# A graph network kernel: the bias in halves at a later place, and the last steps of the first layer's sweep in an order of their own

## The reference, cut to what matters

```python
h = relu(layernorm(x))
msg = h[src] + edge_attr                  # layer 0
m = segment_max(msg * beta, dst)
e = exp(msg * beta - m[dst])
agg = segment_sum(msg * e, dst) / segment_sum(e, dst)
x = x + (agg @ H(phm_rule, W) + bias + h)
h = relu(layernorm(x))                    # layer 1: attention with 4 heads over wx = h @ W.T
x = x + elu(attention(h, W, a, src, dst))
```

## Time and profile before

| what | value |
|---|---|
| median of 3 runs | 2296.75 us (2295.61 to 2296.79) |
| profiled execution, its own time | 2297.38 us |
| its span in the profile | 2295.6 us |
| busy: TensorE, VectorE, ScalarE, GpSimd | 88%, 87%, 59%, 72% of the span |
| layer 0's sweep | about 43 to 1122 us |
| between the layers | 1122 to 1197 us |

### The profile page before, as it was taken

The page is one execution under the profiler, slowest core; times in us unless marked ns, Lnnn a source line. Parts: engine busy times, 40 slices in busy tenths (PEclk is TensorE's granted clock), DMA queues, the critical chain, the costliest instruction groups (busy, mean ns, idle before and its releaser), DMA issues.

```text
span 2295.6 us, 63252 instructions
## 1 busy us (share of the span) xinstructions
PE 2013.3 (88%) x15341; PEld 1806.1 (79%) x15342; DVE 1997.8 (87%) x3846; ACT 1361.5 (59%) x3479; POOL 1648.3 (72%) x1741
## 2 busy tenths in 40 slices
PE   1899999999999999998458999999999999999996
PEld 0778887888887888787458888888888888888885
DVE  7888989898989998999477888888888888888887
ACT  2566666666666666666544555555555555555555
POOL 4777777777777777777427777777777777777772
PEclk9999999999999999999677999999999999999998
DMA  7444454444444444443023333333333333333322
GB/s 209 116 132 135 131 136 131 126 131 135 131 136 131 136 129 128 131 136 99 1 62 61 61 58 59 58 59 59 59 59 59 58 59 59 58 59 58 59 60 67
DMA packets 338046, 214.22 MB, mean 93 GB/s; under 512 B 169981, under 2 KB 304502, under 8 KB 337990
## 3 DMA queue, kind: packets, MB, share of 16 engines
q0 software_dynamic: 53248, 112.57, 20.0%
q1 hardware_dynamic: 282190, 99.72, 17.3%
q10 hardware_dynamic: 2552, 1.28, 0.2%
HBM read 201.37 MB, written 10.29 MB: 92 GB/s over the span
## 4 chain that ended last, share of the span: by engine, by line
POOL 43%; issue 20%; DMA 14%; DVE 10%; PE 6%; ACT 4%; SPq 1%; POOLq 0%; ACTq 0%; DVEq 0%
POOL msg L618 23%; POOL ring_h L582 19%; DMA ring_h<-h_dram,meta_g 11%; PE sums L1229 3%; DVE sums L994 2%; DMA msg<-wx_dram,meta_g 2%; DVE seg_max L999 2%; ACT sums L749 2%; DVE onehot L978 1%; DVE prod L1129 1%; ACT acc L719 1%; PE banks L1238 1%; POOL ring_h L608 1%; PE banks L1245 1%; POOL diff L606 1%
## 5 line engine op out<-in xcount | busy, mean ns | idle before, releaser
L618 POOL DMA_INDIRECT msg<-wx_dram,meta_g x832 | 791.9, 952 | 293.5 <-issue 246.3
L582 POOL DMA_INDIRECT ring_h<-h_dram,meta_g x832 | 788.6, 948 | 260.8 <-issue 248.7
L1229 PE MATMUL sums<-onehot,prod 128*128 128x128 f32 x3312 | 688.2, 291 | 15.1 <-issue 6.1
L1229 PE MATMUL sums<-onehot,wgt 128*128 128x128 f32 x3312 | 674.1, 287 | 0.0
L1229 PEld LDWEIGHTS sums<-onehot,prod 128*128 128x128 f32 x3312 | 535.8, 204 | 47.7 <-issue 47.2
L1229 PEld LDWEIGHTS sums<-onehot,wgt 128*128 128x128 f32 x3312 | 536.7, 204 | 0.0
L719 ACT ACTIVATE acc<-sums 128x1022 f32 x412 | 422.0, 1024 | 0.2
L1238 PE MATMUL banks<-beta_ident,msg 128*128 128x128 f32 x1664 | 243.5, 290 | 91.3 <-DVE msg L1017 89.9
L749 ACT ACTIVATE sums<-ring_h 128x512 f32<-128x512 f32 x208 | 125.1, 602 | 321.7 <-DMA ring_h<-h_dram,meta_g 321.7
L1238 PEld LDWEIGHTS banks<-beta_ident,msg 128*128 128x128 f32 x1664 | 204.8, 194 | 119.7 <-issue 92.8
L1249 PEld LDWEIGHTS banks<-neg_ident,seg_max 128*128 128x128 f32 x1664 | 219.6, 192 | 100.5 <-issue 100.0
(11 more groups left out here) (162 smaller groups left out, 2806.3 us busy)
## 6 DMA issues: line engine op xcount, KB each, us to landing
msg<-in_edge_attr SPq DMA_DIRECT2D x207, 256.0 KB
flags<-flag_dram SPq DMA_DIRECT2D x52, 512.2 KB
ring_h<-h_dram,meta_g POOLq DMA_INDIRECT x832
msg<-wx_dram,meta_g POOLq DMA_INDIRECT x832
window<-wx_dram SPq DMA_DIRECT2D x832, 2.0 KB
wx_dram<-msg SPq DMA_DIRECT2D x13, 272.0 KB, 2.4
nodes<-in_x SPq DMA_DIRECT2D x6, 512.0 KB, 6.8
h_dram<-acc SPq DMA_DIRECT2D x12, 256.0 KB
```

The costliest lines, as they stand in the source:

```text
L582: pool.indirect_dma_start(hg[:, s % HRING, b, :], None, h_dram, bass.IndirectOffsetOnAxis(ap=meta_g[:, s, b:b + 1], axis=0)).then_inc(L0[" ...
L618: pool.indirect_dma_start(msg[:, s, b, :], None, wx_dram, bass.IndirectOffsetOnAxis(ap=meta_g[:, s, b:b + 1], axis=0)).then_inc(L1["gather ...
L1229: ins = pe.matmul(where[:, j, bass.ds(off, P)], what[:, slot, b, :], onehot[:, s, b, :], start=(b == 0), stop=(b == GB - 1), skip_group_ch ...
```

## The change

- The bias addition becomes a helper for either engine. GpSimd adds it to even batches (seven) and VectorE to odd ones (six). GpSimd starts when VectorE has done the last `drop` of layer 0 and no longer waits for `odd_sum`; VectorE starts behind its last product and the sign change of the matrix (L1051), once `odd_sum` is full. `finish0` waits for the half that its batch belongs to.
- The last steps of layer 0 stand in an order of their own on ScalarE, VectorE and TensorE, and the sums of the fourth last and second last group go to `spare_sums0`, banks 2 and 3.
- For that, `row_psum` moves to bank 2 and the result of `unturn0` moves from bank 2 to the bank that `row_psum` had. TensorE writes a row of zeros to bank 3 at the start, and ScalarE waits before the sweep for its own table copies.

```diff
-        row_psum = sums[:, 1, 0, :]
+        shift_psum = sums[:, 1, 0, :]
...
+        row_psum = bank[2]
+        spare_sums0, spare_sums = banks[:, 2:4, :], banks[:, 0:2, :]
...
+        def add_bias(eng, b, done):
+            t = 1 if b == NBAT - 1 else GB
+            tiles = nodes[:, b * GB:b * GB + t, :]
+            eng.tensor_tensor(tiles, tiles, bias_all[:, :].rearrange("p (a d) -> p a d", a=1).to_broadcast([P, t, D]),
+                              ALU.add).then_inc(done, 1)
...
@@ gpsimd
-            pool.wait_ge(odd_sum, NBAT // 2)
             pool.wait_ge(weights_in, 16 * W_DMA)
+            pool.wait_ge(L0["dropped"], NG)
+            straight(NBAT, [(0, even_bias)])
...
@@ scalar
-            sweep_edges(act, [(5, merge0), (0, lift0), (3, weigh0)], until=NG + 4)
+            sweep_edges(act, [(5, merge0), (0, lift0), (3, weigh0)], until=NG - 1)
+            last(weigh0, 3)
+            last(merge0, 5)
+            last(weigh0, 2)
+            last(lift0, 0)
+            last(merge0, 4)
+            last(weigh0, 1)
+            last(merge0, 3, where=spare_sums0)
+            last(weigh0, 0)
+            last(merge0, 2)
+            last(merge0, 1, where=spare_sums0)
             act.activation(spare[:, :], spare[:, :], ACT.Ln)
             last(merge0, 0)
...
@@ vector
-            sweep_edges(dve, [(0, add0), (0, one_hot0), (3, products0), (1, maxima0)])
+            sweep_edges(dve, [(0, add0), (0, one_hot0), (3, products0), (1, maxima0)], until=NG - 1)
+            last(products0, 3)
+            last(maxima0, 1)
+            last(one_hot0, 0)
+            last(add0, 0)
+            last(products0, 2)
+            last(maxima0, 0)
+            last(products0, 1)
+            last(products0, 0)
             dve.tensor_scalar(phm_neg[:, :], ...)
+            dve.wait_ge(odd_sum, NBAT // 2)
+            straight(NBAT, [(0, odd_bias)])
...
@@ tensor
-            sweep_edges(pe, [(4, sums0), (0, turn0), (2, unturn0)])
+            sweep_edges(pe, [(4, sums0), (0, turn0), (2, unturn0)], until=NG - 1)
+            last(unturn0, 2)
+            last(sums0, 4)
+            last(turn0, 0)
+            last(unturn0, 1)
+            pe.wait_ge(L0["onehots"], NG)
+            pe.wait_ge(L0["added"], NG)
+            last(sums0, 3, where=spare_sums0, free=1)
+            last(sums0, 2, free=1)
+            last(unturn0, 0)
+            last(sums0, 1, where=spare_sums0, free=1)
+            last(sums0, 0, free=1)
```

More of the change, by code:

```diff
@@ L213, in gnn_kernel @@
         bank = [banks[:, i, :] for i in range(4)]
-        own_sums, spare_sums = sums[:, 0, :, :], banks[:, 0:2, :]
+        row_psum = bank[2]
+        own_sums = sums[:, 0, :, :]
+        spare_sums0, spare_sums = banks[:, 2:4, :], banks[:, 0:2, :]
         iota_psum = bank[3][:, 0:P]
@@ L259, in gnn_kernel @@
         h_stored = sem("h_stored")
-        bias_added = sem("bias_added")
+        bias_even, bias_odd = sem("bias_even"), sem("bias_odd")
         phm_turned = sem("phm_turned")
@@ L588, in _, with even_bias @@
             pool.wait_ge(even_sum, (NBAT + 1) // 2)
-            pool.wait_ge(odd_sum, NBAT // 2)
             pool.wait_ge(weights_in, 16 * W_DMA)
[L592 to L598, removed]
+            pool.wait_ge(L0["dropped"], NG)
+            def even_bias(b):
+                if b % 2 == 0:
+                    add_bias(pool, b, bias_even)
+            straight(NBAT, [(0, even_bias)])
             def near0(b):
@@ L723, in _ @@
             act.wait_ge(blk_loaded, 16)
+            act.wait_ge(key_out, len(TABLE_BANKS))
             act.wait_ge(h_stored, 16 * NBAT)
@@ L731, in weigh0, with merge0 @@
                     act.wait_ge(L0["summed"], g - (WGT - 1))
-                act.activation(wgt[:, s % WGT, :, :], bank[2][:, :].rearrange("p (b d) -> p b d", b=GB), ACT.Exp)
+                act.activation(wgt[:, s % WGT, :, :], shift_psum.rearrange("p (b d) -> p b d", b=GB), ACT.Exp)
                 if later(g, 1):
                     act.wait_ge(L0["multiplied"], g)
-                act.activation(wgt_psum, bank[2][:, :], ACT.Exp).then_inc(L0["weighed"], 1)
+                act.activation(wgt_psum, shift_psum, ACT.Exp).then_inc(L0["weighed"], 1)
                 act.wait_ge(L0["dropped"], g + 1)
                 act.activation(scale[:, s:s + 1], drop[:, s:s + 1], ACT.Exp).then_inc(L0["factored"], 1)
-            def merge0(g, s, use):
+            def merge0(g, s, use, where=own_sums):
                 if isinstance(g, int) and g == 0:
                     act.wait_ge(odd_sum, NBAT // 2)
-                merge(g, s, use, L0, None)
+                merge(g, s, use, L0, None, where)
             def lift0(g, s, use):
@@ L1046, in _, with odd_bias @@
             link(dve.tensor_copy(iota_psum, iota_f[:, :]))
-            sweep_edges(dve, [(0, add0), (0, one_hot0), (3, products0), (1, maxima0)])
+            sweep_edges(dve, [(0, add0), (0, one_hot0), (3, products0), (1, maxima0)], until=NG - 1)
[7 more added lines that the diff above has]
+            last(products0, 0)
             dve.tensor_scalar(phm_neg[:, :], phm[:, :, :].rearrange("p j b -> p (j b)"), -1.0, None, ALU.mult
                               ).then_inc(phm_turned, 1)
+            dve.wait_ge(odd_sum, NBAT // 2)
+            def odd_bias(b):
+                if b % 2:
+                    add_bias(dve, b, bias_odd)
+            straight(NBAT, [(0, odd_bias)])
             def quotient0(b):
@@ L1065, in finish0 @@
                 dve.wait_ge(mid_out, b + 1)
-                dve.wait_ge(bias_added, b + 1)
+                dve.wait_ge(bias_odd if b % 2 else bias_even, b // 2 + 1)
                 tiles = nodes[0:rows, b * GB:b * GB + t, :]
@@ L1186, in _ @@
             pe.wait_ge(const_ready, 1)
+            pe.matmul(bank[3][:, :], zero_row[0:1, 0:P], zero_row[0:1, :], start=True, stop=True)
             def turn_table(rows_f, first, done):
@@ L1244, in unturn0 @@
                     pe.wait_ge(L0["weighed"], g)
-                pe.matmul(bank[2][:, :].rearrange("p (b d) -> p b d", b=GB), beta_ident[:, :], msg[:, s, :, 0:D],
+                pe.matmul(shift_psum.rearrange("p (b d) -> p b d", b=GB), beta_ident[:, :], msg[:, s, :, 0:D],
                           start=True, stop=False, skip_group_check=True)
@@ L1248, in unturn0, with sums0 @@
                 for b in range(GB):
-                    ins = pe.matmul(bank[2][:, b * P:(b + 1) * P], seg_max[:, s % 2, b * P:(b + 1) * P], neg_ident[:, :],
+                    ins = pe.matmul(shift_psum[:, b * P:(b + 1) * P], seg_max[:, s % 2, b * P:(b + 1) * P], neg_ident[:, :],
                                     start=False, stop=(b == GB - 1), skip_group_check=True)
                 ins.then_inc(L0["unturned"], 1)
-            def sums0(g, s, use):
-                segment_sums(g, s, L0)
+            def sums0(g, s, use, where=own_sums, free=0):
+                segment_sums(g, s, L0, where, free)
             pe.wait_ge(beta_ready, 1)
-            sweep_edges(pe, [(4, sums0), (0, turn0), (2, unturn0)])
+            sweep_edges(pe, [(4, sums0), (0, turn0), (2, unturn0)], until=NG - 1)
[10 more added lines that the diff above has]
+            last(sums0, 0, free=1)
             pe.wait_ge(phm_ready, 1)
```

## The result

The changed kernel takes 2282.52 us (median of 4 runs, 2281.36 to 2283.70); the kernel before takes 2296.77 beside it. The ratio is 0.9937, 95% interval 0.9925 to 0.9950: 14.3 us less, where 13.3 and a time of 2283.5 were forecast. The profiled execution took 2282.86 us with a span of 2281.1.

A forecast was written before the change was run, and what follows sets the result against it. It took GpSimd's gathers to bound the loop and a stalled drop to delay layer 0's end. A gain of 14.1 less 0.8 for the clock, 13.3 us, gave 2284.1 profiled, 2283.5 as median; 8-in-10 range 2281.0 to 2288.5.

The forecast's parts named there:

- What bounds the kernel, and the stall: GpSimd's gathers pace the loop; at layer 0's end its bias additions hold one VectorE drop, a 12.9 us stall.
- The layout of the new queues: Layer 0's last steps, laid out from undisturbed rows: merges end at 1108.1 instead of 1122.2, gaining 14.1 us at full clock.
- The clock: TensorE's gaps in layer 0's tail cost half a slow stretch, 0.8 us; bounds 0 and 8.2 us.
- Without any reordering the stall's end alone would give about 11: Layer 0's tail in old order: addition of 207 at 1088.8, then the old 22.45 us to the merges' end; 11 us.
- the order is worth nothing: Rival: reordering layer 0's last steps gains nothing, only the stall's 11 us remain, 2285.8 us; chance 0.08.
- The bias at its new place costs zero: Both bias halves end before quotient work at 1112.3, the odd half by 1107.9 at worst; cost zero.
- Slower through the swapped banks: Rival: swapped PSUM banks lengthen each loop step by 0.38 us per group, 2301.4 us or more; chance 0.03.
- the stall that moves: Rival: VectorE and GpSimd delay each other over the bias halves until quotient work is late, 2291 us; chance 0.04.

The follow-up runs named there:

- e1: Kernel before plus one line: GpSimd waits for the drop of group 207 before its thirteen bias additions; ratio 0.9941.
- e2: Changed kernel's order and banks, with all thirteen bias additions on GpSimd at the old place, right behind the gathers; ratio 0.9999.
- e4: Changed kernel with its new order but one pair of banks for the sums, as before; ratio 0.9965, median 2293.56 us.
- e11: Kernel before with the bias early on GpSimd, each addition waiting by semaphore for the one before; ratio 0.9943.
- e12: Kernel before with the bias early on GpSimd and an empty instruction between its additions; ratio 0.9998.
- e3: Changed kernel with all thirteen bias additions on GpSimd at the late place, none on VectorE; ratio 0.9937, median 2287.57 us.
- e9: The merged order: changed kernel with merge 202 back at its old place, spare banks kept, table load behind the last weighing; ratio 0.9923, median 2282.78 us.
- e6: Changed kernel unedited, on the chip where the kernel before took 3366 us; ratio 0.9975 (0.9938 to 1.0012).

## Why the prediction held, point by point

- *What bounds the kernel, and the stall.* Right, and shown by e1 and e2: the bias behind the gathers held the drop, and taking it away shortens the interval by 14.2 us, leaving it gives nothing.
- *The layout of the new queues.* With the 0.45 us by which this trace runs late, the addition of 207 was put at 1091.55 and came at 1091.57; the sums of 204 at 1095.05 and 1095.05; the end of the unturn of 207 at 1100.55 and 1100.54; merge 205 at 1101.65 and 1101.67; the end of the merges at 1108.5 and 1108.45. Rows of undisturbed steps, start to start, carry such a sum far better than a difference of two totals.
- *The clock.* A term mis-sized: 0.8 us taken, nothing measured, the clock is 1.00 up to 1105. That is most of the 1.0 us between forecast and result. The worry wasn't idle: the clock fell behind a wait of 2.98 us in e4, and behind one of 2.05 us, before the last set of sums, in the kernel before and in e11. It did not fall behind the same wait in e1 and e12; what decides stays open.
- *"Without any reordering the stall's end alone would give about 11."* Wrong, and with it the rival built on it: e1 gives 14.2. The step that failed is the old 22.45 us from the addition of 207 to the merges' end, which I took over whole. It held a start at half speed and a last set of sums at half speed; in e1 the same stretch has neither and is 1110.33 - 1090.75 = 19.6 us. The start is the stall's doing: from the addition of 207 to the sums of 204 it is 5.24 us in the kernel before and 3.49 in e1. The last set (1.1 us) is not shown to be: it was at half speed in e11 too, which has no stall, and at full speed in e12, which has it. So the forecast of the new kernel was right by its rows, but the 3 us that it gave to the order belonged to the stall and to the clock, and it took e1 to see that. In the same way *the order is worth nothing* was true as a statement and false as a forecast of 2285.8. In the kernel before, the start of the sums of 204, and TensorE from the last set of sums on (columns as in the earlier trace rows):

```profile
1105.01 0.39 PE L1229 MATMUL sums<-onehot,prod 128*128 128x128 f32 x2
```

```profile
1117.00:1121.00 4.00, 3.15 (x16) 2.89 (x16) 0.00 (x0) 1.91 (x5) 0.00 (x0) 0.60 0.00 0
```

- *The bias at its new place costs zero.* Right. GpSimd's additions started at 1096.48 (1096.25 forecast with the shift), products beside them took 0.69. The even half ended at 1104.7, 0.7 later than laid out, mostly because it met the odd one; the odd half ended at 1107.7, short of the bound of 1108.4. Halving wasn't needed for it (e3). In the merged order it may be: thirteen additions from 1098.0 would end near 1113.1, and the quotient work starts at 1110.8. That was not run.
- *Slower through the swapped banks, and the stall that moves.* Neither shows: TensorE is busy 46.57 of 50 us in the loop, against 47.12, and the quotient work keeps its 4.24 us.

## What to carry to other kernels

When an instruction of no size takes microseconds and waits for nothing, look at what runs beside it on the other engines: here a wait of one line, or a wait between GpSimd's additions, was worth all that a new order, a second pair of banks and a split over two engines came with. Time each part of such a change alone, the cheapest first. When you lay out what is left after a stall, don't take over the stretch behind it as it was: part of it ran at a clock that the stall had brought down. And when two traces differ by more than the medians do, look at the clock in each before you give the difference to the edit (e4).

## What was not expected of the hardware

- The drop (three operands in SBUF, one element per partition) did not get in between two additions of GpSimd that ran back to back, at either length tried: 13.16 us held beside additions of 1.25 us, 14.51 beside additions of 0.44. A wait for the addition before, 0.13 us each, suffices. An empty instruction on GpSimd makes no gap.
- Other VectorE instructions do get in. The sign change, one operand in SBUF, took 0.37 us in e3 in the midst of the additions and 0.92 in e9, against 0.22 alone. The bias additions on VectorE, two operands in SBUF, were held for about one of GpSimd's: in e9 the longest took 1.77 us instead of 0.68, and GpSimd's 1.70 instead of 1.26. These go with one instruction held per lock, as the Trainium skill has it (SBUF — State Buffer, section "Who interferes with whom"); the drop doesn't. The lines of e9:

```profile
L331 POOL TENSOR_TENSOR nodes<-nodes,bias_all x7: 899/1260/1704, 1098.0 to 1105.8; 128x512 f32<-128x512 f32 x6, 128x128 f32<-128x128 f32 x1
...
L331 DVE TENSOR_TENSOR nodes<-nodes,bias_all x6: 678/807/1768, 1102.9 to 1108.4; 128x512 f32<-128x512 f32 x6
```

  Whether it is the drop's form, its third operand or its size of one element that makes the difference stays open; no run here varied them. The runs show who was held and for how long, not by what.
- One chip took 3366 us for what the others did in 2297 to 2301, at a mean TensorE clock of 0.79. The low clock is not shown to be the cause. From 400 to 1000 us of e6 TensorE is busy only 439 of the 600 us (557 in the changed kernel), and ScalarE's weighing alone waits 168.5 us for a releaser that the profile calls remote, for which it never waits in that stretch of the changed kernel. Waits of e6 (us in total, times, longest us):

```profile
POOL ring_h L590 <- ACT banks L756: 178.4, 44, 6.1
ACT wgt L739 <- remote: 168.5, 28, 8.2
```
